# Cross attention and the mixture of experts of a two-layer decoder, joined into one stage on one core

## What is computed

```python
# L1 cross attention: q is x, k and v are the context, all read as (batch, 256, 512):
# 8 heads of 32 rows, 512 queries, 512 keys
qk = jnp.einsum('bhdq,bhdl->bhql', qh, kh) * scale
sm = jax.nn.softmax(qk, axis=-1)
ret = jnp.einsum('bhql,bhdl->bhdq', sm, vh)
x = _layernorm(x + gamma * ret)
# L1 experts: 8 experts of rank 16, the 2 best of a row are used
gates = jax.nn.softmax(x @ Wr + br + bonus, axis=-1)
topk_vals, topk_idx = jax.lax.top_k(gates, 2)      # then normalised to sum 1, one-hot weights w
h = jax.nn.relu(jnp.einsum('btd,edr->betr', x, Wd) + bd)
out = einsum(w, jnp.einsum('betr,erd->betd', h, Wu) + bu)
x = _layernorm(x + out)
```

## Time and profile before

| | us |
|---|---|
| median of 3 runs | 2086.15 (2080.94 to 2093.19) |
| the profiled execution | 2083.66 |
| its span, first to last instruction | 2081.9 |

### The profile page before, as it was taken

How to read it: one execution, slowest core, us unless ns; L and a number is a source line. 1 busy time by engine, 2 the same in 40 slices (tenths; PEclk the granted TensorE clock), 3 DMA queues, 4 the chain that set the end, 5 groups by cost and what they waited for, 6 DMA issues and landing times. The chain is left out here.

```text
span 2081.9 us, 33021 instructions
## 1 busy us (share of the span) xinstructions
PE 1846.4 (89%) x12272; PEld 1503.4 (72%) x12272; DVE 1249.2 (60%) x2330; ACT 920.4 (44%) x2376; POOL 288.0 (14%) x347
## 2 busy tenths in 40 slices
PE   6979999999976799999999996799997498889966
PEld 5868999998964588888888985677775365555543
DVE  3446444444434565546555536788887288878847
ACT  2224333333323343333333223666666288878811
POOL 0000000000002111111111001333343111121001
PEclk9989999999997799999999998999998699999988
DMA  3122000000013231111101013000010675556234
GB/s 104 45 97 72 21 21 21 21 21 21 10 48 101 66 97 47 36 31 41 46 19 34 11 41 121 11 31 32 31 42 21 182 179 136 153 140 149 68 114 142
DMA packets 86253, 136.62 MB, mean 66 GB/s; under 512 B 9480, under 2 KB 25480, under 8 KB 86096
## 3 DMA queue, kind: packets, MB, share of 16 engines
q1 hardware_dynamic: 86096, 134.52, 22.3%
HBM read 79.88 MB, written 21.05 MB: 48 GB/s over the span
## 5 line engine op out<-in xcount | busy, mean ns | idle before, releaser
L1164 PE MATMUL yp<-ccy,toep 128*128 128x288 f32 x640 | 182.4, 436 | 19.5 <-POOL ccy L892 13.4
L1965 ACT ACTIVATE e_p<-e_s_ps,e_nb 128x512 f32<-128x512 f32 x256 | 175.0, 696 | 51.6 <-DVE e_nb L2013 49.5
L2013 DVE TENSOR_REDUCE e_nb<-e_s_ps 128x2 f32<-128x1024 f32 x128 | 155.8, 1218 | 54.3 <-PE e_s_ps L2090 53.5
L1442 ACT ACTIVATE p<-p,nb,rq 128x128 f32<-128x128 f32 (+1 forms) x256 | 137.0, 541 | 94.5 <-DVE nb L1539 94.5
L2100 PE MATMUL e_t_ps<-ident,e_p 128*128 128x128 f32 x1024 | 148.7, 284 | 24.7 <-DVE e_pT L2020 13.2
L1164 PEld LDWEIGHTS yp<-ccy,toep 128*128 128x128 f32 x640 | 126.5, 206 | 55.7 <-POOL ccy L892 14.8
L2100 PEld LDWEIGHTS e_t_ps<-ident,e_p 128*128 128x128 f32 x1024 | 120.8, 146 | 62.5 <-issue 52.9
L80 PE MATMUL q_ps<-a_xt_hi,wq_hi 128*128 128x256 f32 x512 | 151.7, 296 | 4.1 <-DVE wo_lo L112 4.1
L1062 DVE SCALAR_TENSOR_TENSOR hm<-gu_ps,us_col,sg 128x256 f32<-128x256 f32 x88 | 42.3, 481 | 182.3 <-ACT sg L971 182.3
L82 PE MATMUL q_ps<-a_xt_hi,wq_lo 128*128 128x256 f32 x512 | 146.5, 286 | 0.0
L81 PE MATMUL q_ps<-a_xt_lo,wq_hi 128*128 128x256 f32 x512 | 146.4, 286 | 0.0
(11 more groups left out here) (277 smaller groups left out, 5122.1 us busy)
## 6 DMA issues: line engine op xcount, KB each, us to landing
x_after<-n_r SPq DMA_DIRECT2D x24, 512.0 KB, 3.0
toep<-padded_kernels SPq DMA_DIRECT2D x32, 256.0 KB, 3.5
qs<-e_xh SPq DMA_DIRECT2D x64, 128.0 KB, 2.5
qs<-e_xl SPq DMA_DIRECT2D x64, 128.0 KB, 2.6
ks<-e_ch SPq DMA_DIRECT2D x64, 128.0 KB, 2.6
ks<-e_cl SPq DMA_DIRECT2D x64, 128.0 KB, 2.6
x<-x_after SPq DMA_DIRECT2D x12, 512.0 KB, 4.7
x<-in_x SPq DMA_DIRECT2D x8, 512.0 KB, 4.1
```

Source lines behind the costliest of these rows:

```text
L1164: last = pe.matmul(yp[:, lo % 2, 0:NCOL], toep[h % 2][:, (lo - li) * P:(lo - li + 1) * P], ccy[h % 2][:, li, 0:NCOL], start=(li == 0), sto ...
L1442: act.activation(p[n % 3][:, h, part[t]], p[n % 3][:, h, part[t]], ACT.Exp, bias=nb[i][:, t, h:h + 1], scale=rq[u][:, t:t + 1], accum_out= ...
L1965: act.activation(pr[i][:, a, :], s_ps[i][:, a, :], ACT.Exp, bias=nb[i][:, a:a + 1], accum_out=sums[t][:, j, q:q + 1]).then_inc(e_done, 1)
L2013: dve.tensor_reduce(nb[i][:], s_ps[i][:], AX.X, ALU.max, negate=True).then_inc(nb_done, 1)
```

## The change

One stage, `l1_cross_and_experts`, takes the place of both. A **unit** is one head by 128 queries: one score matmul into one of four banks, one maximum over 512, one exponential, three units later four transposes, copied to SBUF by ACT (even units) or DVE (odd units). A batch has 32 units, u % 4 being the head within a half, and so the group of `stacked` that it needs. The products with the values are made for four units together (16 matmuls of 128 columns in place of 4 of 512 for each head group). There are 9 x 32 steps: in each, every engine does its part of one unit and what the table of steps adds for that number:

```diff
+                for b, step, u in steps():          # PE
+                    if b < B:
+                        scores(u)
+                    v = behind(u, 3)
+                    if v is not None:
+                        turn(v)
+                    v = behind(u, 8)
+                    if v is not None and v % HT == 0:
+                        values(v // HT)
+                    if step == 2 and b:
+                        spread_sums(b - 1, 1)
+                    if step in (12, 14) and b:
+                        turn_x(b - 1, (step - 12) // 2)
+                    if step == 16 and b:
+                        project(b - 1)
+                    if step == 18 and b < B:
+                        spread_sums(b, 0)
+                    if step in (20, 22) and b + 1 < B:
+                        turn_context(b + 1, (step - 20) // 2)
+                    if step == 25 and b:
+                        turn_hidden(b - 1)
+                    if step in (28, 30) and b:
+                        out(b - 1, (step - 28) // 2)
...
+                    if step == 1 and b + 1 < B:      # ACT, after exps(u) and copy_t(u - 3)
+                        round_hi(b + 1, "ch")
+                    if step == 3 and b:
+                        spread(b - 1, 1)
+                    if step == 5 and b + 1 < B:
+                        round_hi(b + 1, "xh")
+                    if step in (13, 15) and b:
+                        turned(b - 1, (step - 13) // 2)
+                    if step == 18 and b:
+                        exponential(b - 1)
+                    if step == 19 and b < B:
+                        spread(b, 0)
+                    if step in (21, 23) and b + 1 < B:
+                        context(b + 1, (step - 21) // 2)
+                    if step == 26 and b:
+                        hidden(b - 1)
...
+                take_lo(dve, 0, "cl")                # DVE
+                dve.wait_ge(w_loaded, 64)
+                dve.tensor_scalar(bias[:, 0, 0:E], bias[:, 0, 0:E], BONUS, None, ALU.add).then_inc(prepared, 1)
+                dve.wait_ge(prepared, 3)
...
+                    if step == 2 and b >= 2:
+                        apply(b - 2, mv6, rstd6, rstd6_done, y6_done)
+                    if step == 5 and b:
+                        scale_out(b - 1, 1)
+                    if step == 7 and b:
+                        statistics(b - 1, added5, st5, st5_done, mv5, mv5_done)
+                    if step == 10 and b:
+                        apply(b - 1, mv5, rstd5, rstd5_done, y5_done)
+                    if step == 17 and b:
+                        shift(b - 1)
...
+                    if step in (29, 31) and b:
+                        add_experts(b - 1, (step - 29) // 2)
+                    if step == 31 and b:
+                        statistics(b - 1, added6, st6, st6_done, mv6, mv6_done)
```

A batch's normalised rows stay in SBUF (`e_r`, two buffers): they are the experts' input and the residual, so the store and two loads of x_after_5 are gone. The residual of cross attention is added by POOL (at steps 5 and 21) instead of DVE. All that is not a score, a transpose of a unit or a value product goes through the one bank `m_ps`, ten times a batch, each new use waiting until the last has been read:

```diff
+                def m_bank(*freed):
+                    if read:
+                        pe.wait_ge(*read.pop())
+                    read.append(freed)
```

SP's list at the start of the stage is now:

```diff
+                load(1)
+                stack(0)
+                residual(0)
+                    sp.dma_start(wrd[:, :, 0:E], wr.rearrange("(k p) n -> p k n", p=P)).then_inc(w_loaded, 16)
+                sp.dma_start(wrd[:, :, E:], wdn.rearrange("(k p) n -> p k n", p=P)).then_inc(w_loaded, 16)
+                sp.dma_start(bias[:, 0, 0:E], br.partition_broadcast(P)).then_inc(w_loaded, 16)
+                sp.dma_start(bias[:, 0, E:], bd.partition_broadcast(P)).then_inc(w_loaded, 16)
```

More of the change, by code:

```diff
@@ L2175, in l1_experts @@
         numbers = sb("f_numbers", [P, 1, 1, E])
[L2176 to L2178 removed]
+        xT = sb("f_xT", [P, KT, S])
         lh = sb("f_lh", [P, T, E + E * R])
@@ new lines, in l1_cross_and_experts, with steps, place, behind @@
+        LAST = UNITS * B
+        def steps():
+            for b in range(B + 1):
+                for step in range(UNITS):
+                    yield b, step, UNITS * b + step
+        def place(u):
+            b, rest = divmod(u, UNITS)
+            t, rest = divmod(rest, TILE)
+            return b, t, rest // HT, rest % HT
+        def behind(u, count):
+            return u - count if 0 <= u - count < LAST else None
+        def in_buffer(eng, sems, b):
+            eng.wait_ge(sems[b % 2], 16 * (b // 2) + 16)
@@ L2269, in body @@
-                def body(b, u, first, last):
-                    if not last:
-                        turned(b + 1, 1 - u)
-                    if not first:
-                        hidden(b - 1, 1 - u)
-                    exponential(b)
-                turned(0, 0)
-                over_batches(act, body, lambda b, u: hidden(b - 1, 1 - u))
+                    if b:
+                        act.wait_ge(o_mm, T * b)
+                    act.activation(hwT[:], m_ps[:, 0:S], ACT.Copy).then_inc(hT_done, 1)
@@ new lines, in hidden @@
+                    act.activation(wT[:], m_ps[:, S:2 * S], ACT.Copy).then_inc(hT_done, 1)
+                round_hi(0, "ch")
+                act.wait_ge(g_loaded, 16)
+                for r in range(2):
+                    context(0, r)
+                round_hi(0, "xh")
+                for b, step, u in steps():
+                    if b < B:
+                        exps(u)
+                    v = behind(u, 3)
+                    if v is not None and v % 2 == 0:
+                        copy_t(v)
+                    if step == 1 and b + 1 < B:
[14 more added lines that the diff above has]
+                        hidden(b - 1)
@@ new lines, in scores, with turn @@
+                def scores(u):
+                    b, t, q, j = place(u)
+                    if u % UNITS < HT:
+                        pe.wait_ge(stacked[j], 16 * 8 * (b + 1))
+                    if u >= SB:
+                        pe.wait_ge(e_done, u - SB + 1)
+                    pe.matmul(s_ps[u % SB][:], qs[b % 2][:, t, j, q * P:(q + 1) * P], ks[b % 2][:, t, j, :],
+                              start=True, stop=True).then_inc(s_mm, 1)
+                def turn(u):
+                    pe.wait_ge(e_done, u + 1)
+                    if u >= 2:
+                        pe.wait_ge((ta_done, td_done)[u % 2], u // 2)
+                    for k in range(LB):
+                        last = pe.transpose(t_ps[u % 2][:, k, :], pr[u % EB][:, k * P:(k + 1) * P], core.ident[:])
+                    last.then_inc(t_mm, 1)
@@ new lines, in values @@
+                def values(g):
+                    b, t, q, _ = place(HT * g)
+                    pe.wait_ge(ta_done, 2 * g + 2)
+                    pe.wait_ge(td_done, 2 * g + 2)
+                    if q == 0 and g:
+                        pe.wait_ge(o_scaled, T * b + t)
+                    if q == 0 and t == 0:
+                        pe.wait_ge(vt_done, 2 * b + 2)
+                    for k in range(LB):
+                        for j in range(HT):
+                            e = t * P + j * CX
+                            last = pe.matmul(v_ps[j * CX:(j + 1) * CX, q * P:(q + 1) * P], vt[b % 2][:, k, e:e + CX],
+                                             pT[g % 2][:, j, k, :], start=(k == 0), stop=(k == LB - 1),
+                                             skip_group_check=True, tile_position=(0, j * CX))
+                    last.then_inc(pv_mm, 1)
```

698 lines of the change are left out of this document (280 added, 418 removed).

## The result

| | us |
|---|---|
| before, median of 4 runs | 2086.38 (2080.94 to 2093.19) |
| changed, median of 4 runs | 2113.36 (2111.89 to 2117.89) |
| ratio, 95% interval | 1.0137 (1.0116 to 1.0158) |
| changed, the profiled execution and its span | 2111.89, 2110.1 |

The change makes the kernel 1.4% slower. The forecast was 2097, 11 us over the time before; 27 were measured. In what follows one of e10's ten executions, which fell into a slow state (4902.69 us), is left out of its median.

A forecast was written before the change was run, and what follows sets the result against it. It saw waiting as the old bound and one bank's hand-overs as the new: batch 0 ends at 1704, seven batches of 50.3 less 1.0, last experts 37.2, span 2092.9, 11.0 over 2081.9, so 2097 us; range 2030 to 2120.

The forecast's parts named there:

- the likeliest case: Hand-overs of the one bank m_ps set the batch's pace: centred on 2097 us, 2083 to 2111, chance 0.50.
- The main mechanism: Each m_ps use waits for its reader behind exponential and unit's copy on ACT: 3.45 us for two steps, engines need 1.8.
- The wait for the weights: At the stage's start DVE's first maximum waits for the experts' weights, 7.55 us from first issue to landing, until 1667.4.
- 12 to 14: Hand-over of m_ps after the rows' transposes: 3.45 us plus 0.85 because DVE still owes units 11 and 12, 4.3.
- 25 to 28: Three steps between uses of m_ps where PE's own work binds (scores, transposes, values): 3.36 us.
- 30 round to 12: From the m_ps use at step 30 through statistics (5.06 us), then DVE-bound steps 0 to 10 (15.05) and a 0.1 signal.
- With a copy every other unit that is 0.90. ... Four banks remove the loop: Plain units: DVE and ACT each need 0.90 us; four score banks remove the score loop, so 0.90 against 1.07 before.
- DVE's work binds steps 0 to 10: Maxima, copies, normalisings, scaling, statistics and reciprocals on DVE take 14.6 us, 15.05 with POOL's e_xl; PE 11, ACT 12.
- The hand-overs don't bind: Rival: already filled banks cover the wait and DVE's 41.1 us a batch sets the pace, 2028 us; chance 0.15.
- Half of each wait is covered: Rival: hand-overs in a batch cost half their wait, 45.7 us a batch, 2062 us; chance 0.15.
- The falling clock: Rival: PE's gaps in steps 12 to 30 lower the clock, 33 us in all, 2130 us; chance 0.08.
- POOL hold DVE's normalising at step 2: Rival: POOL's e_cl starts first and blocks DVE's normalising, 2.3 us a batch, 16 in all, 2113 us; chance 0.10.

The follow-up runs named there:

- e10: Changed kernel with PE issuing the next unit's score ahead of the use of m_ps, only in steps that use that bank: 2081.93 us.
- e9: The kernel before, unchanged, profiled a second time: span 2087.5 us, where its first profile had 2081.9.
- e4: Changed kernel with DVE's wait for the experts' weights and the bias addition moved from ahead of the first maximum to step 16 of batch 1: 2104.83 us.
- e11: Changed kernel with the next score issued ahead of transposes and values on PE, only in steps that don't use m_ps: 2107.62 us.
- e16: Changed kernel with ACT copying a unit's transposes (even units) ahead of the exponential of its step: 2095.26 us.
- e14: Changed kernel with DVE's normalising of the experts' rows at step 2 cut to 8 of 512 columns, except the last batch: 2114.11 us.
- e12: Changed kernel with m_ps readers first, scores one unit ahead and late weights' wait (2060.83 us), plus experts' normalising moved from DVE to POOL: 2059.55 us.
- e1: Changed kernel with the copies on ACT that free m_ps put ahead of the exponential and the unit's copy: 2093.62 us.
- e3: Changed kernel with two banks in turn for the hand-overs and three instead of four for the scores: 2087.42 us.
- e5: Changed kernel with readers of m_ps first on ACT and scores one unit ahead on PE: 2069.05 us.
- e17: Changed kernel with m_ps readers, then unit copies, ahead of exponentials on ACT, scores one unit ahead on PE, weights' wait late: 2045.47 us.
- e13: Changed kernel with ACT's two roundings of a batch cut to 8 of 512 columns from the second batch on: 2126.77 us.

## Why the prediction was right or wrong

**The sign held, the size did not.** The kernel got slower, as forecast, and 2113.36 lies in the wide range of 2030 to 2120, but outside the 2083 to 2111 of the likeliest case, and the rise was 27 us and not 11. The main mechanism held as a description: each use of the bank is handed over by the chain that the prediction wrote down, and the waits that it named as proof (PE for `f_xT`, `e_vt`, `e_rb` on ACT) are in the trace, though only two are of its 1 to 2 us; the others last 0.4 to 0.6.

**Where the span's end of 2110.1 came from.** The prediction's terms add up to 2092.3 (it states 2092.9). Against them:

- 2.65 us: the stage begins later (POOL's `e_scale` at 1632.41, in the first profile of before at 1629.76). The stages ahead are the same; this lies within the scatter of the experiments (e9).
- 1.6 us: from there to the first maximum 39.3 us, forecast 37.6. The wait for the weights took 9.3 us from the first issue (1662.18 to 1671.46), not 7.55. The step was right; e4 sized it at 8.5 us in the median.
- 6.5 us: from the first maximum to batch 0's experts' power 92.4 us, forecast 85.9. 2.4 of it is batch 1, which took 51.7 like the others (from its use of the bank in step 2 at 1714.26 to the next at 1765.99): 1.4 is the period's, and 1.0 the normalising that it lacks and that saved nothing. 4.1 is batch 0, nearly all of it in steps 22 to 31, plain units at 1.23 for which 0.90 were taken (12.4 us, forecast 8.7). Steps 0 to 17 took 20.5, forecast 20.4, and that is luck: the forecast had 4.1 for roundings and a low clock on top of its 0.90 a unit. e11 (3.3 less) and e16 (5.9 less, 2.2 of it the period's) show the loop that the prediction overlooked.
- 7.4 us: six more batches of 51.53 on average, forecast 50.3.
- minus 0.4: the last batch, 36.8 to the forecast 37.2. It ran mostly at the low clock, as the prediction took it. That it fits so closely is partly luck: in e4, whose last batch has the same work, it took 39.0.

**The batch, term by term.** 12 to 14: 3.55 (forecast 4.3); 14 to 16: 3.52 (3.45); 16 to 18: 4.03 (4.32); 18 to 20: 4.26 (4.15); 20 to 22: 3.53 (3.45); 22 to 25: 3.69 (3.36); 25 to 28: 4.22 (3.36); 28 to 30: 3.69 (3.68); 30 round to 12: 21.23 (20.21). Six of the nine hold within 0.35 us; 12 to 14 was forecast 0.75 too long. The excess lies in 25 to 28 (0.86) and 30 to 12 (1.02): stretches where the prediction saw an engine's own work as the bound, PE's in the one and DVE's in the other, and no wait. That the whole batch is off by only 1.4 owes something to the 12 to 14 that was taken too long.

**The step that failed** is "With a copy every other unit that is 0.90. ... Four banks remove the loop". The prediction costed one loop, of score, maximum, exponential and the next score. It left out the one through the transposes: PE's transposes of a unit wait for the copy of the unit two before, which on ACT stands behind the exponential of its step, and the next score stands behind those transposes. Moving the copy forward (e16) brought plain units from 1.23 to 1.05 and took 2.2 us off each batch, 1.1 of it in the two stretches with the excess of 1.9; what the other 0.8 there is stays open. That DVE's work binds steps 0 to 10, the prediction's reason for 15.05, was wrong at least for the normalising at step 2: e14 and e12 took it away and nothing moved. What DVE does there later (statistics, normalising at step 10) was not tried. A maximum also occupies DVE for 0.65 us (two in 1884.46 to 1885.75), not 0.60.

**The size of the hand-overs was misread.** The prediction's rival without them had DVE's 41.1 in place of 50.3. Removing them where they could be removed (e1, e3) gave 2.8 to 3.2. It had written "PE can't fetch the next score earlier, since its wait stands ahead of it"; that is so in this list and no property of the bank, and e10, which moves only that score, took off 4.6 us. More is lost because DVE has nothing to reduce meanwhile than because the bank is held, and the two are mostly the same wait (e5).

**The rivals.** "The hand-overs don't bind" was wrong in the changed kernel: its 41.1 a batch (the terms given for DVE add up to 40.7) appeared in no run, and e17 with 43.9 came nearest. "Half of each wait is covered" was wrong too. The falling clock did not happen in the changed kernel's steady batches (granted clock 1.00), nor did POOL hold DVE's normalising at step 2 (1.00 us); at step 10, beside `e_xl`, normalising took 1.24, where the prediction had allowed 0.45 more. e13 shows both rivals real: the second missed by 0.1 us.

**The time before.** The prediction checked its method on two steps of 4.29 us, which lie in the slower pace of the old kernel (44.2 a batch). That the same code also runs at 38.2 was in the trace, in the powers between the two of the earlier trace rows.

## What to carry to other kernels

When a helper bank or buffer is handed between engines in hand-ordered lists, first ask what stands behind each wait on its engine: here issuing the next unit's input ahead of the wait was worth more (4.6 us a batch) than a second bank (3.2). On an engine that serves a loop, put what another engine waits for ahead of what only fills a buffer, and try each engine apart, since the same move gained 2.2 us a batch on ACT and lost 2.4 on DVE. A cost per unit is the longest of all loops through it, the one by way of the freeing copy too, and not the largest engine share.

## What was not expected of the hardware

- Less work made the kernel slower: shortening ACT's rounding from 1.06 to 0.22 us brought a POOL subtraction onto a DVE `tensor_scalar`, which then took 3.05 us (two of 512 columns) or 2.66 (two of 8 columns), against 1.00 and 0.47.
- The granted clock fell to 0.50 inside a steady batch of e13, after 2.28 busy of 4.00 us on PE; in the changed kernel stretches with 2.44 and 1.97 of 4.00 kept 1.00.
- A `tensor_scalar` of 512 columns in SBUF took 2.3 us on POOL and 0.5 on DVE; an add took POOL 1.27.
- The kernel before runs its batches at two paces, about 44.2 and 38 to 40 us, and changed over at different batches in its two profiled executions. One batch more at the slow pace is 5 us, an estimate from these paces of what it adds to the spread of its times.
